# Reloading the attention weights during the last expert instead of after the barrier, in an eight-core attention and mixture-of-experts layer

## What is computed

```python
def _L0_attn_ref(x, norm_w, Wq, Wk, Wv, Wqf, Wkf, Wout):
    h = rmsnorm(x, norm_w)
    q = (h @ Wq); k = (h @ Wk); v = (h @ Wv)          # 16 heads of 64
    q_phi = taylor_feature_map(q @ Wqf)               # 1 + 16 + 136 features
    k_phi = taylor_feature_map(k @ Wkf)
    lin = linear_attention_causal(q_phi, k_phi, v)
    win = sliding_window_attention(q, k, v)
    return x + jnp.concatenate([lin, win], axis=-1) @ Wout

x = _layernorm(x + _L0_attn_ref(x, ...))
# every expert: h0 = x w0 + b0, h1 = x w1 + b1, out = (h0 * silu(h1)) w2 + b2,
# weighted by the softmax of the two largest gate logits
x = _layernorm(x + _L0_ffn_ref(x, ...))
```

## Time and profile before

| | |
|---|---|
| median of three runs | 9645.14 us |
| time of the profiled execution | 9645.67 us |
| its span, slowest core (core 4) | 9643.8 us |
| spans of the eight cores | 9635.0 to 9643.8 us |
| busy: TensorE, ScalarE, VectorE, GpSimd | 73%, 28%, 19%, 9% |
| mean granted TensorE clock | 0.820 |
| chain of work that ended last: TensorE, ScalarE, GpSimd, DMA | 71%, 8%, 7%, 2% |

### The profile page before, as it was taken

One profiled execution on the slowest core, in us unless ns is written; L12 is line 12 of the kernel. 1 busy time (PEld: TensorE's weight loads), 2 busy tenths in 40 slices (PEclk: granted clock), 3 DMA queues, 4 the chain that ended last, 5 costly groups with the idle time before them and its releaser, 6 DMA issues.

```text
span 9643.8 us, 104822 instructions; the slowest of 8 cores (9635.0 to 9643.8 us)
## 1 busy us (share of the span) xinstructions
PE 7023.7 (73%) x37091; PEld 3420.8 (35%) x37091; DVE 1831.5 (19%) x4145; ACT 2674.8 (28%) x3877; POOL 869.8 (9%) x1530
## 2 busy tenths in 40 slices
PE   3344899998334489999734448999973444999997
PEld 1222344443122234444312224444431222444443
DVE  2222211111222221111122221111112222111111
ACT  1222233333122223333312222333341222333333
POOL 1211000000121100000012110000001211000000
PEclk8565899999656599999965659999986565999998
DMA  3000645442300063545230006364513001536451
GB/s 57 1 9 2 100 60 88 74 72 37 70 1 9 6 100 56 89 72 75 33 70 1 9 10 98 54 93 68 79 32 67 1 5 18 90 58 97 61 87 38
DMA packets 243920, 493.80 MB, mean 51 GB/s; under 512 B 14032, under 2 KB 14032, under 8 KB 243408
## 3 DMA queue, kind: packets, MB, share of 16 engines
q0 software_dynamic: 225424, 453.02, 31.5%
q1 hardware_dynamic: 17984, 34.09, 1.2%
HBM read 923.32 MB, written 16.78 MB: 97 GB/s over the span
## 4 chain that ended last, share of the span: by engine, by line
PE 71%; ACT 8%; POOL 7%; issue 5%; DVE 4%; DMA 2%; another core or an unknown queue 2%; DVEq 0%; ACTq 0%; POOLq 0%; SPq 0%
PE pb L90 39%; PE pbA L90 16%; PE pbB L90 12%; ACT arena L90 7%; POOL arena L90 7%; PE pT L90 4%; DVE arena L90 2%; DMA arena<-x 1%; ACT t L90 1%; DVE smal L90 1%; DMA out<-t 0%; DVE t L90 0%; ACT smal L90 0%; DVEq L89 0%
## 5 line engine op out<-in xcount | busy, mean ns | idle before, releaser
L90 PE MATMUL pb<-arena 128*128 128x512 bf16 (+2 forms) x19328 | 3890.1, 364 | 259.0 <-ACT arena L90 211.7
L90 PEld LDWEIGHTS pb<-arena 128*128 128x128 bf16 (+1 forms) x19328 | 1848.8, 103 | 2271.7 <-issue 337.3
L90 ACT ACTIVATE arena<-pb,arena 128x512 bf16<-128x512 f32 x2048 | 1407.0, 687 | 2153.1 <-PE pb L90 2056.6
L90 PE MATMUL pbB<-arena 128*128 128x512 bf16 (+1 forms) x5504 | 1089.0, 343 | 1105.1 <-POOL arena L90 974.3
L90 PE MATMUL pbA<-arena 128*128 128x512 bf16 x6656 | 1548.2, 394 | 133.9 <-DMA arena<-wout 86.6
L90 DVE TENSOR_TENSOR arena<-arena 128x512 bf16<-128x512 bf16 (+13 forms) x1536 | 654.7, 426 | 3131.7 <-ACT arena L90 2924.9
L90 PEld LDWEIGHTS pbB<-arena 128*128 128x128 bf16 x5504 | 527.9, 104 | 1656.9 <-issue 1173.6
L90 PEld LDWEIGHTS pbA<-arena 128*128 128x128 bf16 x6656 | 669.2, 101 | 982.5 <-issue 255.2
L90 PE MATMUL pT<-idbf,arena 128*128 128x128 bf16 (+1 forms) x3072 | 415.7, 303 | 808.6 <-DVE arena L90 564.6
L90 ACT ACTIVATE arena<-pT 128x512 bf16<-128x512 bf16 (+1 forms) x576 | 368.3, 639 | 1267.7 <-PE pT L90 1244.4
L90 DVE TENSOR_TENSOR t<-t,arena 128x1024 f32<-128x1024 f32 x256 | 313.7, 1225 | 1593.0 <-ACT arena L90 1593.0
(11 more groups left out here) (84 smaller groups left out, 1744.5 us busy)
## 6 DMA issues: line engine op xcount, KB each, us to landing
arena<-w2t POOLq DMA_DIRECT2D x32, 4352.0 KB, 32.7
arena<-w0t POOLq DMA_DIRECT2D x64, 2048.0 KB, 18.7
arena<-w1t POOLq DMA_DIRECT2D x64, 2048.0 KB, 29.3
arena<-x SPq DMA_DIRECT2D x32, 512.0 KB, 4.0
arena<-wout POOLq DMA_DIRECT2D x4, 4096.0 KB, 72.3
out<-t SPq DMA_DIRECT2D x4, 4096.0 KB, 14.1
arena<-wq POOLq DMA_DIRECT2D x4, 2048.0 KB, 19.6
arena<-wk POOLq DMA_DIRECT2D x4, 2048.0 KB, 33.3
```

Source lines behind the costliest of these rows:

```text
L90: r = getattr(e, meth)(*args, **kw)
```

## The change

The loads of the attention weights for the next quarter are issued behind the eighth expert's code and ahead of the last layer norm, and the four after the barrier are gone. Each waits for the last matmul of expert 7 that reads the bytes it overwrites. Wout is loaded in two halves: the first lies where w1 was, the second where w2 was. The semaphore `dw` and the barrier stay.

```diff
             wtok = load_expert(e + 1, lastuse["w00"], lastuse["w01"],
                                lastuse["w10"], lastuse["w11"],
                                lastuse["w2"], lastuse["b"])
+            else:
+                last_e = lastuse
@@
         self.lr["pb3"] = h1_free
+        if q + 1 < self.nq:
+            self.tk_wq = self.load_mat(self.wq_s, self.wq_h, 8,
+                                       after=[last_e["w01"]])
+            self.tk_wk = self.load_mat(self.wk_s, self.wk_h, 8,
+                                       after=[last_e["w01"]])
+            self.tk_wv = self.load_mat(self.wv_s, self.wv_h, 8,
+                                       after=[last_e["w11"]])
+            wo3h = self.wout_s.rearrange("p (s w) -> p s w", s=16)
+            t_wo1 = self.OP("gpsimd", "dma_start", out=wo3h[:, 0:8, :],
+                            in_=self.wout_h[0:1024, :].rearrange("(s p) w -> p s w", p=128),
+                            after=[last_e["w11"]], inc=("dw", 16))
+            t_wo2 = self.OP("gpsimd", "dma_start", out=wo3h[:, 8:16, :],
+                            in_=self.wout_h[1024:2048, :].rearrange("(s p) w -> p s w", p=128),
+                            after=[last_e["w2"]], inc=("dw", 16))
+            self.tk_wo = t_wo2
         self.load_act(self.SET_NLE)
@@
             self.pl.op("sync", "nop", after=[self.store_tok])
             self.pl.barrier()
-            self.tk_wq = self.load_mat(self.wq_s, self.wq_h, 8)
-            self.tk_wk = self.load_mat(self.wk_s, self.wk_h, 8)
-            self.tk_wv = self.load_mat(self.wv_s, self.wv_h, 8)
-            self.tk_wo = self.load_mat(self.wout_s, self.wout_h, 16)
```

## The result

The changed kernel took 9516 to 9524 us in five executions, against 9637 to 9652 in eight of the kernel before; the ratio is 0.9868 with a 95% interval of 0.9849 to 0.9887, so 1.3% less time.

What follows compares the result with a forecast made beforehand. TensorE's matmul chain bounds the kernel, with DMA in it: at three boundaries it waits for weights, which also slow x loads. Removing 130.4 us from 9645.67 gives 9515.2 us, 1.35% less; range 9496 to 9568.

Steps and rivals of the forecast that it cites:

- the first sentence of the sum: Starting level of the forecast: the profiled execution's 9645.67 us, 0.5 above the median of the runs shown.
- The wait of TensorE and the stretched x loads: At three superchunk boundaries, projections start 44.39, 43.18 and 42.87 us earlier; two thirds TensorE's wait, one third x loads.
- rival A: At the boundaries, x loads stay slow and only TensorE's wait for wout goes: 83.9 us less, 9562; chance 0.07.
- The Trainium skill's price of one DMA: x loads: about 2.0 us plus bytes at 436 GB/s, 3.2 us per 512 KB; sum 6 us more, 9509.
- The landing of the loads: Five weight loads issued from 2335.3 in the last expert land by 2403.6, at the upper bound 2411.8, before the store.
- The cost beside other work: Loads beside TensorE's output stage (29.5 us) and ScalarE's layer norm (54 us) cost nothing.
- Rival C: Last layer norm: the loads stretch ScalarE's passes by 2.6, +25 us a boundary, 9721, slower than before; chance 0.02.
- Rival D: At the boundaries the transfer was hidden anyway, something else taking over TensorE's wait: 9645; chance 0.02.
- Rival B: Loads come late and share DMA engines with the store and first x load: some 20 us a boundary, 9575; chance 0.05.
- The Trainium skill's rule on VectorE and GpSimd's descriptors: VectorE's two-port modes shut out GpSimd's descriptor generation; could delay loads by 3.7 us in the norm, sum unchanged.
- The clock: Projections at the boundaries: granted clock 0.50 before, 0.95 over them; no difference taken, half a microsecond each either way.

Runs made afterwards that it cites:

- the first series: Follow-up runs on one chip with the kernel before beside them: changed kernel again 9516.41 us, kernel before 9636.97 us, one execution each.

## Why the prediction was right or wrong

*The time itself* was wrong: 9515 us with a range of 9496 to 9568 was forecast, and the median of ten executions is 9916.28 us. The step that failed is the first sentence of the sum, which starts from 9645.67, "0.5 above the median of the runs shown". It took this for the level of the kernel, although the three runs shown reached 10581.24, and it put executions at a lower granted clock at nothing: no term, no chance. The ten executions showed in its place a median of 10205.45 us for the kernel before, with six of ten over 10000 us, and seven of ten of the changed kernel at 9806 to 10701 us. Their mean granted clocks went down to 0.726, where the profiled execution had 0.825. The cause of the lower clock was not studied; both kernels have it, and the 289 us between the two medians are not the effect of the change.

*The size of the change* was right: 130.4 us less was forecast, 128 are measured as the mean over the cores' spans, 120.6 between the two executions of the first series (9636.97 and 9516.41); the ratio is 0.9868 against a forecast of 0.9865 (9515.2 / 9645.67). The five times given in the result lie inside the range, 1 to 9 us above the forecast.

*The wait of TensorE and the stretched x loads* were the two parts, and both went. Forecast was a chain of 27.56 us from first transposes to projections; measured 28.10, 27.50 and 28.46 at the three boundaries of the slowest core, 27.38, 26.92 and 27.47 on core 4. The saving of the two cores that were slowest, counted up to the last quarter's experts, is 119.5 us on core 2 and 138.1 on core 4; no term of the sum holds such a difference between cores, and its cause is not shown. The split was forecast through rival A as 83.9 for the wait alone and thus 46.5 for x. Measured were 74 and 46. That rival A's 9562 us came out as 9562.67 for the kernel with own semaphores is luck, since that series started 9 us lower. Rival A itself is refuted: the gaps in the changed kernel are 3.6 to 5.0 us. The Trainium skill's price of one DMA (DMA: Bandwidth & Descriptors, Anatomy of one DMA), which the prediction set beside the x loads, is by its heading for loads issued from GpSimd, and SyncE issues these. The trace has them landing in 3.4 to 5.9 us, with a median of 3.5 (core 4) and 3.8 (core 2).

*The landing of the loads* was forecast 68.3 us after the first issue (2403.6 - 2335.3). On the slowest core the second half of Wout was issued at 2371.14 and took 39.0 us, so it landed at 2410.1, 70.1 us after the first issue at 2340.05; at the other two boundaries it was 69.3 and 68.3 us, and 64.8 to 66 on core 4. Taking the price from the expert loads, the same size from the same queue in the same stage, was the right choice between the two rates. (From its own numbers the loads end 17 us before the store and 31 before the barrier at best, not 18 and 32.)

*The cost beside other work* was forecast as nothing. The output stage took 29.5 us in both, and the norm 51.63 us (2373.22 to 2424.85) against 51.62 before (2369.19 to 2420.81). Rival C is refuted by this, and by the kernel without reloads, which is no faster. Rival D is refuted by the gain itself.

*Rival B* was the right mechanism with a margin that the change keeps. Loads that are 30 us late make the store longer by 10 us, with the x gaps untouched, 11 a boundary; I had priced it at 20. The Trainium skill's rule on VectorE and GpSimd's descriptors (SBUF - State Buffer, Who interferes with whom) was not put to a test by these runs: POOL's issues took 0.88 to 0.90 us and the first load landed in 17.8 us in the median, with VectorE at work for only 3.7 of the norm's 54 us.

*The clock* moved nothing here: the projections had 0.95 granted in either kernel, and took 43.18 us against 43.67.

## What to carry to other kernels

A load that makes an engine wait can also slow the other loads beside it: look at the gaps of the small transfers in the same stretch, since here they were over a third of the gain. Here, moving the transfers paid only where they moved to a stretch in which the DMA engines had time to spare, so compare the DMA share of the two windows before counting on it; inside one full stretch the earlier issue changed only who waits. And ask what each wait stands for: one semaphore over several loads waits for the last of them, and separating them brought 74 us (weights) and 76 us (x), each more than half of what the move brought.

## What the runs showed of the hardware

The store on SP's queue and the weights on POOL's share the DMA engines: a 4096 KB store that lands in 12.1 to 14.6 us by itself, in either kernel, took 21.5 to 24.8 us beside the weight loads (cores 0 and 4 of the two kernels that issue them late), and the gaps that wait for an x load are 3.6 to 5.0 us in the changed kernel and 8.3 to 10.3 beside the weight loads. What I had not expected is how closely it balances (core 4, first boundary): counted from the start of the store, the loads were issued 14.6 us behind it before and 0.45 us behind it in the kernel that issues them with the store, and the projections started 91.1 and 89.8 us behind it.
